# Mix stage of a two-layer block: gates of the output a piece later, silu of x, Exp and Ln in slots of their own, the later side steps moved behind them

## What is computed

```
xn = layernorm(x);  x = x + attention(xn) + switch_ffn(xn)      # layer 0: 16 heads with rope; 16 experts of capacity 320
xn = layernorm(x);  x = x + mamba(xn) + mx_linear(xn)           # layer 1

mamba:   xi, z = xn @ in_proj
         u     = silu(causal_conv4(xi) + b)                     # 512 channels
         dt_low, B, C = u @ x_proj
         delta = softplus(dt_low @ dt_proj + dt_b)
         h[t]  = exp(delta*A) * h[t-1] + delta*B*u              # 16 states a channel
         y     = sum_n(h*C) + u*D
         out   = (y * silu(z)) @ out_proj
mx_linear: blocks of 32 scaled by their maximum, rounded to a grid of 6 bits, times the weight rounded alike, plus bias
```

## Time and profile before

| | |
|---|---|
| runs, us | 2226.01, 2225.51, 2225.57; median 2225.57 |
| the profiled execution, us | 2220.31 |
| its span, first to last instruction, us | 2218.5 |
| busy, us (share of the span) | PE 1719.3 (77%), DVE 1488.8 (67%), ACT 1004.6 (45%), POOL 942.7 (42%) |
| DMA | 223.79 MB, mean 101 GB/s |
| mix stage | from about 1130 us on: DVE's first scan starts at 1130.76, the last gate at 2195.18 |

### The profile page before, as it was taken

The page is one execution under the profiler, slowest core; times in us unless marked ns, Lnnn a source line. Parts: engine busy times, 40 slices in busy tenths (PEclk is TensorE's granted clock), DMA queues, the critical chain, the costliest instruction groups (busy, mean ns, idle before and its releaser), DMA issues.

```text
span 2218.5 us, 21659 instructions
## 1 busy us (share of the span) xinstructions
PE 1719.3 (77%) x6696; PEld 757.2 (34%) x6696; DVE 1488.8 (67%) x1744; ACT 1004.6 (45%) x1542; POOL 942.7 (42%) x676
## 2 busy tenths in 40 slices
PE   7499999999999999994727696685967859677645
PEld 7253535262625353531302141321413224132202
DVE  6446464546464646372068796987979888797995
ACT  3125252525343443434334746556465554656541
POOL 2700000000000000002288786877777877677761
PEclk9899999898989898997858796786977869777756
DMA  4553635262625354423141331423214142231420
GB/s 180 203 88 104 102 103 95 97 108 96 109 96 93 111 79 126 68 51 104 42 159 48 111 118 58 146 84 138 109 59 156 53 152 95 77 133 39 152 86 9
DMA packets 103055, 223.79 MB, mean 101 GB/s; under 512 B 12641, under 2 KB 64994, under 8 KB 99282
## 3 DMA queue, kind: packets, MB, share of 16 engines
q1 hardware_dynamic: 99922, 214.69, 34.1%
q0 software_dynamic: 3072, 8.37, 1.1%
HBM read 169.56 MB, written 53.48 MB: 101 GB/s over the span
## 4 chain that ended last, share of the span: by engine, by line
PE 18%; DVE 16%; issue 8%; ACT 8%; DVEq 1%; DMA 1%; POOLq 1%; POOL 1%; ACTq 0%; SPq 0%
DVE ps L1460 11%; PE ps L1559 9%; DVE work L1466 5%; PE ps L1584 3%; PE ps L1552 2%; ACT ps L1333 2%; PE ps L1571 2%; PE ps L1567 1%; ACT L1333 1%; ACT u L1276 1%; ACT inputs L1304 1%; ACT sz L1314 1%; ACT e_rows L1252 1%; PE ps L1591 0%; ACT L1306 0%
## 5 line engine op out<-in xcount | busy, mean ns | idle before, releaser
L1192 POOL TENSOR_TENSOR work<-rep,bc 128x1024 f32<-128x1024 f32 x256 | 600.2, 2365 | 166.2 <-PE ps L1584 143.1
L1460 DVE TENSOR_TENSOR_SCAN ps<-ps,work 128x1024 f32<-128x1024 f32 x256 | 585.2, 2286 | 119.5 <-ACT ps L1333 119.5
L1333 ACT ACTIVATE ps<-rep,a_neg 128x512 f32<-128x512 f32 x512 | 331.1, 682 | 311.9 <-DVE work L1466 310.1
L708 DVE TENSOR_REDUCE m<-ps 128x1 f32<-128x512 f32 x512 | 328.0, 686 | 158.8 <-PE ps L814 156.0
L631 ACT ACTIVATE prob<-ps 128x1024 f32<-128x1024 f32 x256 | 257.3, 1021 | 224.5 <-PE ps L838 222.7
L1584 PE MATMUL ps<-work,pick 128*32 128x512 f32 x1024 | 182.1, 792 | 180.7 <-DVE work L1466 180.7
L1466 DVE TENSOR_TENSOR work<-ps,bc 128x1024 f32<-128x1024 f32 x256 | 308.6, 1206 | 0.0
L572 POOL TENSOR_TENSOR m_parts<-m,nil 128x16 bf16<-128x16 f32 x32 | 7.0, 220 | 603.2 <-DVE m L708 603.2
L1559 PE MATMUL ps<-xn_t,in_taps 128*128 128x510 f32 (+3 forms) x512 | 232.4, 608 | 8.7 <-ACT x L1322 5.6
L814 PE MATMUL ps<-k_st,q_st 96*128 96x512 bf16 x512 | 200.3, 436 | 30.9 <-DVE m L708 24.7
L838 PE MATMUL ps<-q_st,k_st 99*128 99x512 bf16 x512 | 166.6, 423 | 1.0 <-DVE e_rest L684 0.3
(11 more groups left out here) (176 smaller groups left out, 2087.4 us busy)
## 6 DMA issues: line engine op xcount, KB each, us to landing
rep<-rep_rows SPq DMA_DIRECT2D x128, 512.0 KB, 6.1
w<-in_w SPq DMA_DIRECT2D x32, 1024.0 KB
bc<-bc_rows SPq DMA_DIRECT2D x32, 512.0 KB, 4.0
rep_rows<-inputs SPq DMA_DIRECT2D x32, 512.0 KB, 5.2
qk_parts<-parts SPq DMA_DIRECT2D x96, 128.0 KB
q_st<-qk_parts SPq DMA_DIRECT2D x96, 128.0 KB, 10.4
k_st<-qk_parts SPq DMA_DIRECT2D x96, 128.0 KB, 11.2
dispatch<-zeros SPq DMA_DIRECT2D x4, 1280.0 KB, 10.5
```

The lines of the kernel that those rows point to most:

```text
L708: nc.vector.tensor_reduce(m[:, g % 2, qt, 2 * pair + i:2 * pair + i + 1], ps[:, S0 + i, :], AX.X, ALU.max).then_inc(s_reduced, 1)
L1192: nc.gpsimd.tensor_tensor(work[:, n % WS, :, :], rep[:, g % RS, 2 * h:2 * h + 2, 1, :], bc[:, k, 0, :].unsqueeze(1).broadcast_to([P, 2, SE ...
L1333: e = nc.scalar.activation(state(n)[:, i, :], rep[:, g % RS, 2 * h + i, 0, :], ACT.Exp, scale=a_neg[:, c, 2 * h + i, k:k + 1])
L1460: nc.vector.tensor_tensor_scan(s, s, work[:, n % WS, :, :].rearrange("p i t -> p (i t)"), 0.0, ALU.mult, ALU.add).then_inc(state_ready, 1)
```

## The change

The tables: silu of x gets piece 17 for itself (it shared piece 16 with the last x copy). The projection of B and C, its copy and the dt steps come one piece later. `softplus` is split into `exponents` (piece 24) and `softplus` (the Ln, piece 25); both had been in piece 22 behind the last dt copy. z comes one piece later on PE and two on ACT, the turned quantised tokens one later on PE and two on ACT, silu of z one later; it stands between the two copies of quantised tokens now. POOL's four scalings of the inputs come one piece later, where the third and fourth share piece 31. In the code, all four gates come one piece later: 2, 10, 18, 26.

```diff
-PE_AT = {"turn_x": (0, 1), "out": (2, 3, 5, 6), "w": 1, "first_quant": (2, 3), "x": (7, 9, 11, 13), "bc": 16, "dt": (18, 19, 20, 21),
-         "z": (22, 23, 24, 25), "turn_quant": (26, 27)}
-ACT_AT = {"normalise": 0, "turned": (1, 2), "out": (5, 8), "w": 2, "first_quant": (3, 4), "x": (10, 12, 14, 16), "silu_u": 16, "step": 9,
-          "rows": 18, "dt": (19, 20, 21, 22), "softplus": 22, "z": (24, 25, 26, 27), "quant": (28, 29), "silu_z": 29, "weigh": 24}
+PE_AT = {"turn_x": (0, 1), "out": (2, 3, 5, 6), "w": 1, "first_quant": (2, 3), "x": (7, 9, 11, 13), "bc": 17, "dt": (19, 20, 21, 22),
+         "z": (23, 24, 25, 26), "turn_quant": (27, 28)}
+ACT_AT = {"normalise": 0, "turned": (1, 2), "out": (5, 8), "w": 2, "first_quant": (3, 4), "x": (10, 12, 14, 16), "silu_u": 17, "step": 9,
+          "rows": 19, "dt": (20, 21, 22, 23), "exponents": 24, "softplus": 25, "z": (26, 27, 28, 29), "quant": (30, 31), "silu_z": 30, "weigh": 24}
 DVE_AT = {"max": 2, "binade": 6, "statistics": 26}
-POOL_AT = {"down": 9, "grid": 14, "up": 17, "gather": 23, "add": 27, "input": 28, "root": 31}
+POOL_AT = {"down": 9, "grid": 14, "up": 17, "gather": 23, "add": 27, "input": 29, "root": 31}
...
-                def softplus(f):
+                def exponents(f):
                     act.drain()
                     nc.scalar.activation(du, du, ACT.Exp, scale=-1.0)
+
+                def softplus(f):
                     act.drain()
                     nc.scalar.activation(du, du, ACT.Ln, bias=1.0).then_inc(log_ready, 1)
...
+                        if q == ACT_AT["exponents"] + late:
+                            exponents(f)
                         if q == ACT_AT["softplus"] + late:
                             softplus(f)
...
-                        if b and q == 1:
+                        if b and q == 2:
                             gate_y(b - 1, DC - 1)
                         for c in range(DC - 1):
-                            if q == PER_CHUNK * (c + 1) + 1:
+                            if q == PER_CHUNK * (c + 1) + 2:
                                 gate_y(b, c)
```

More of the change, by code:

```diff
@@ L1356, in _ @@
                     take_dt(0, c, DT_FIRST[c])
+                exponents(0)
                 softplus(0)
```

## The result

| | before | after |
|---|---|---|
| runs beside each other, us | 4, median 2225.79 (2225.51 to 2227.15) | 4, median 2195.30 (2195.00 to 2200.92) |
| profiled execution, its span, us | 2220.31, 2218.5 | 2195.57, 2193.8 |
| first scan of the mix stage | 1130.76 | 1131.01 |
| first scan to end of span ("mix stage") | 1087.7 | 1062.8 |
| sequence 0, scan 0 to scan 0 | 139.0 | 137.9 |

The ratio is 0.987, 95% interval 0.985 to 0.989: faster, by 30.5 us between the medians and by 24.7 between the two profiled spans. The forecast was 2210, range 2196 to 2223; the time lies 0.7 under the range. The gain was forecast as 15.1 against the profiled execution.

A forecast was written before the change was run, and what follows sets the result against it. DVE sets the mix stage's time. Gains of 21.8 (sequences 1 to 5) and 2.2 (sequence 6), less 5.7 (sequence 0) and 3.15 (sequence 7), make 15.1: 2220.31 becomes 2205.2, plus 5.3 to the median, rounded to 2210; range 2196 to 2223.

The forecast's parts named there:

- X: Time origin in each sequence of the mix stage: the start of PE's first tap matmul, 1437.37 in the kernel before.
- POOL never the releaser: POOL's input scalings and drives at a sequence's end: costed at nothing, with 4 us of cover.
- given back at the x copy: x stage: the 1.36 us wait saved at gate 0 was to be lost again at ACT's x copy.
- the end of a sequence: Middle sequences: the next one starts at X+99.5 instead of 105.4, 5.9 us earlier.
- z3: Last z matmul on PE, behind 3.2 us of idle time: taken at 3.78 us, or 1.98 at full clock.
- the output's delay: Later gate 3 starts the output projection 2.4 us later, so scan 6 loses 1.55 us in a middle sequence.
- The side steps of DVE: DVE's gates, statistics, maxima and binades between scans: some 10 us of each sequence.
- sequence 7: Last sequence: its output projection waits for the gate alone, starts 3.32 us later, and 3.15 us are lost.
- The step that failed: Sequence 0: fourth x copy unchanged at 1215.92, last quantised-token copy 4.0 to 6.7 us later; 5.7 taken as lost.
- The output delay costs nothing: Rival: ACT's copy of the output has room, so 12.4 us come back, giving 2198; chance 0.13.
- TensorE falls to its low clock: Rival: seed, sum and dt matmuls run slowly, costing 2.5 us in six sequences: 2225, no change; chance 0.11.
- The dt copies slip a piece: Rival: a dt column misses its slot, later copies come up to 4.5 us later: 2237, slower; chance 0.11.

The follow-up runs named there:

- e1: The kernel before with only the gates one piece later, nothing else changed; 2206.91 us, ratio 0.993.
- e2: The changed kernel with all four gates back in pieces 1, 9, 17 and 25; 2213.6 us, ratio 0.995.
- e3: The changed kernel with gate 3 alone back in piece 1 of the next sequence; 2183.69 us, ratio 0.981.
- e7: The changed kernel with the expert rows weighed in piece 22 instead of 24; 2196.24 us, ratio 0.987.
- e8: The changed kernel with Exp back in one piece with Ln, both in piece 25; 2203.28 us, ratio 0.990.
- e4: The changed kernel with PE's sum of piece 24 ahead of z block 1, except in sequence 0; 2179.68 us, ratio 0.980.
- e6: The changed kernel with the side steps of sequence 0 later by 4 pieces instead of 5; 2198.42 us, ratio 0.987.
- e5: The changed kernel with gate 3 back in piece 1 and the sum of piece 24 ahead of z block 1; 2162.74 us, ratio 0.973.
- e10: e5 with the expert rows weighed in piece 22 except in sequence 0, there 24; 2166.15 us, ratio 0.972.

## Why the prediction came out as it did

**Right: the mechanism and nearly each place in a middle sequence.** Forecast and measured in sequence 2: scans 17 and 18, 1.5 and 2.5 against 1.31 and 2.56; scans 25 and 26, 1.6 and 2.5 against 1.39 and 2.47; gate 2 at X+77.5 with 3.5 against X+76.7 with 3.1 to 3.9; gates 0 and 1 without waits; the fourth x copy at X+32.1; POOL never the releaser. The wait of 0.89 at scan 15, which came with the later gates (e1 has it too, e2 has not), stands only in the words "given back at the x copy", not in the list of waits. That the total came out does not show that its parts were understood: the expectation of e1 gave the gates next to nothing, and alone they give 18.6 of the 23.8 in sequences 1 to 5.

**Mis-sized: the end of a sequence.** It was put at X+99.5 and came at X+98.0, in sequence 2. z3 was taken at 3.78, "the value behind idle time", and took 3.08 and 2.40 behind 3.19 of idle time; scan 31 waited 1.13, not 1.9. Against this, the output's delay was priced at 1.55 and cost by turns 1.4 and 2.65 (X stands 32.49 behind scan 0 of sequence 2 and 33.74 in sequence 3, for 31.09 before). The side steps of DVE were taken as they were, and one of them (L1445) took 0.8 more. A sequence became 131.7 long on average, against 132.2: five gave 23.8 where 21.8 was forecast. Sequence 6 gave 3.5 for 2.2; sequence 7 lost 3.3 for 3.15, and e3 shows that all of it is gate 3.

**The step that failed: sequence 0.** "The fourth x copy is again at 1215.92", and "waits saved earlier in this sequence buy nothing, as this chain sets its end". The chain does set the end, but its place was taken as fixed. It hangs on a wait of PE in the first tap block, for a read of DVE (3.15 before, 1.20 after). The copy came 3.7 earlier behind the first scan: 2.0 because a DVE step behind the moved gate 0 took 0.70 in place of 2.67, a term that the prediction had at nothing, and 1.7 because half a tap block ran at the high level, which it also did in e2 without the moved gates. Behind the copy, the fourth dt copy ended 1.5 earlier than forecast, and the way from Ln to the last copy was 1.6 shorter. So 5.7 lost became 1.1 gained. Of the 10 us by which the sum fell short (15.1 for 25.1, adding the rows of the table), this is 6.8. With the gates back (e2), sequence 0 loses 4.5, near the 5.7; by the rows 2.0 of the 5.6 between e2 and after belong to the gates, and most of the rest to matmuls at the low level. So part of the 6.8 is luck: where PE's matmuls in this chain ran at the high level and where at the low one was not forecast and differs between runs (z block 2 took 1.98 in after, 3.78 in e2, e7 and e8).

**The anchor.** I added 5.3 to reach the median, since before's profiled execution lay that far below its own. After's lay 0.3 above its median. That is the other 5 of the 14.7 between forecast and result: scatter of a few us that neither trace explains. The prediction's own range was added up wrongly: 3.5 to 5.6 a sequence and 4.0 to 6.7 at sequence 0 give 9.9 to 23.1 gained, so 2202.5 to 2215.7 and not 2204 to 2217. Neither holds the result.

**The rivals.** "The output delay costs nothing" gave the time nearest to the result (2198) for the wrong reason: e3 excludes it. "TensorE falls to its low clock" named nothing new: in sequence 2 of the kernel before, three of the four dt matmuls already took 2.07, though the first, which the earlier trace rows shows and the prediction held against this rival, took 1.12. After the change two take 2.07, and z1 takes 3.78 in both kernels. The next sequence began 7.4 earlier after X than before, 6.8 in sequence 3, so the low level cost no more than the sum already held. The Trainium skill (TensorE: Matmul & The Clock Gate, "Why this matters for your kernels") warns of this drop behind idle gaps. The 3.78 behind 8.93 idle us agrees; the rule did not decide the case, since that block was slow before too. "The dt copies slip a piece" did not happen: the fourth copy ended at X+59.4, where the sum had it at 59.6 and the turning point at 62.2.

## What to carry to other kernels

Where a consumer that sets the pace waits a few microseconds for a finished sum, moving it one step later in its own order can be worth more than speeding up the producer; then look at what the later consumer in turn releases, and leave the one that feeds a chain (here gate 3) where it was. When the start or end of a pipeline is set by another chain than its middle, follow that chain back to its first wait (here PE's, for a read of DVE, in the first tap block) before saying that waits saved earlier buy nothing. Where two moments move together, such as gate 1's shorter wait and the earlier fourth copy, look whether the first thing that is early comes ahead of the supposed cause. And put first in a producer's order what the next wait needs: one sum moved ahead of one z block (e4) brought 15.6 us between the medians, more than gate 3's return with 11.6.

## What was not expected of the hardware

- Sequences 1 to 5, of equal work, took 132.4 to 132.7 and 130.4 to 130.5 by turns, and so again in e6 and e8; in e4 127.3 and 128.7. The two differ in TensorE's granted level over the first output columns (3.45 and 1.03 against 3.78 and 1.91 for the same matmuls) and around gate 2 (waits of 3.1 and 3.8); a sequence that begins one way leads to one that begins the other. With gate 3 earlier (e3) all are alike. That the clock's state is what is handed on is the reading that fits; no run tested it by itself.
- The same z block, 0.69 idle us behind the same slow block, took 1.98 in e5 and 3.78 in e10. In e4, within one execution, it took 1.98 in sequences 1, 3 and 5 and 3.78 in 2 and 4. A small shift of the work around it decided, so a block's time taken from one order can be off by 1.8 in another.
- DVE's two `binade` instructions (before L1440 and L1443, after L1445 and L1448; f32 or int32, 128x1024) ran 182 times in the 13 traces. 57 took 0.68 to 0.88. The other 125 took 1.01 to 2.91, and each of these ended 0.55 or 0.56 after the end of one of POOL's drives, whenever it had begun. That DVE stands still there until POOL's drive is done is the reading that fits; no run took the drives away. It makes a DVE step's place beside POOL's work worth up to 2.2 us.
- A table load (1.28) starts within 0.1 us of the activation before it ends: 1468.20 behind a decay that ends at 1468.14, and silu starts at 1469.50: 1.36 for the whole switch. The Trainium skill (ScalarE: Activation LUTs, "What ACT_TABLE_LOAD costs") has the same 1283 ns and adds a drain of about 1380 ns; no such drain shows in the timeline of ACT here.
